# A four-layer mixer on one core: the linear-attention half's second feature block, LN1 turn, state copy and running sum move to other steps

## What is computed

```python
x = x + linear_attention(layernorm(x))   # 16 heads; q, k through softplus + 1e-6; causal running sums
x = x + ffn(layernorm(x))                # a recurrence over batches: c = f * c + i * g, then tanh(x Wo + c Uo)
x = x + softmax_attention(layernorm(x))  # causal, ALiBi
x = x + ffn(layernorm(x))
```

## Time and profile before

| what | before |
|---|---|
| median of 3 runs | 2518.53 us (2517.84 to 2527.41) |
| the profiled execution, its own time | 2519.05 us |
| its span, first to last instruction | 2517.2 us |
| PE busy | 2119.3 us (84%) |
| DVE busy | 1696.5 us (67%) |
| ACT busy | 1264.0 us (50%) |
| POOL busy | 773.3 us (31%) |
| mean granted TensorE clock | 0.938 |

### The profile page before, as it was taken

How to read it: one execution, slowest core, us unless ns; L and a number is a source line. 1 busy time by engine, 2 the same in 40 slices (tenths; PEclk the granted TensorE clock), 3 DMA queues, 4 the chain that set the end, 5 groups by cost and what they waited for, 6 DMA issues and landing times.

```text
span 2517.2 us, 58448 instructions
## 1 busy us (share of the span) xinstructions
PE 2119.3 (84%) x24737; PEld 1214.4 (48%) x24838; DVE 1696.5 (67%) x3770; ACT 1264.0 (50%) x2040; POOL 773.3 (31%) x654
## 2 busy tenths in 40 slices
PE   4678888979798885669789999999999999998953
PEld 2556555656556553334345455444544545444432
DVE  7666565665646454447878888787887887777337
ACT  3323434242434221215666676766677666766723
POOL 1234141423332011162425254243452432412110
PEclk9879999999999997878999999999999999999987
DMA  4001010101101011143323134141331412213063
GB/s 148 18 18 58 29 51 18 52 25 45 43 10 52 2 52 55 47 136 108 93 75 114 51 79 135 42 123 58 85 119 44 120 50 77 77 36 106 31 234 134
DMA packets 131540, 179.28 MB, mean 71 GB/s; under 512 B 9120, under 2 KB 95136, under 8 KB 131280
## 3 DMA queue, kind: packets, MB, share of 16 engines
q1 hardware_dynamic: 129104, 175.02, 22.6%
q10 hardware_dynamic: 2176, 0.52, 0.1%
HBM read 97.40 MB, written 77.59 MB: 70 GB/s over the span
## 4 chain that ended last, share of the span: by engine, by line
PE 64%; DVE 23%; ACT 7%; issue 4%; POOL 2%; DMA 0%; SPq 0%; DVEq 0%; POOLq 0%; ACTq 0%
PE general L897 11%; PE general L583 10%; PE out_of_heads L771 9%; DVE maxima L1462 8%; PE scores L726 6%; PE general L569 4%; PE general L908 4%; PE general L549 3%; PE turned_scores L740 3%; PE out_of_heads L657 3%; PE out_of_heads L667 2%; PE scores L615 2%; PE general L557 2%; PE out_of_heads L791 1%; PE scores L675 1%
## 5 line engine op out<-in xcount | busy, mean ns | idle before, releaser
L1462 DVE TENSOR_REDUCE maxima<-scores 128x1 f32<-128x512 f32 (+3 forms) x1536 | 796.1, 552 | 228.5 <-PE scores L702 117.2
L1095 ACT ACTIVATE probs_turned<-turned_scores 128x512 f32<-128x512 f32 x1152 | 680.0, 601 | 353.5 <-PE turned_scores L702 180.0
L726 PE MATMUL scores<-k_stacks,q_stacks 59*128 59x512 bf16 (+3 forms) x1536 | 444.7, 335 | 59.8 <-DVE maxima L1462 54.0
L740 PE MATMUL turned_scores<-q_stacks,k_stacks 61*128 61x512 bf16 (+3 forms) x1536 | 436.5, 329 | 9.4 <-ACT probs_turned L1095 9.4
L726 PEld LDWEIGHTS scores<-k_stacks,q_stacks 59*128 59x128 bf16 x1536 | 124.0, 94 | 286.8 <-DVE maxima L1462 220.0
L1792 POOL TENSOR_TENSOR ln_low<-ln 128x512 bf16<-128x512 f32 x128 | 140.8, 1107 | 278.5 <-DVE ln L1444 278.5
L1771 POOL TENSOR_SCALAR ln<-x_for_attention,ln_mean_var,ln_rstd 128x256 f32<-128x256 f32 x104 | 129.0, 1251 | 184.7 <-DVEq L1551 96.8
L1023 ACT ACTIVATE gate_tanhs<-general,feature_vectors 128x512 f32<-128x512 f32 x96 | 66.0, 687 | 204.6 <-PE general L583 200.3
L1707 POOL TENSOR_TENSOR state_low<-state_doubled,state_high 128x2048 bf16<-128x2048 f32 x14 | 57.0, 4069 | 363.0 <-ACT state_high L1029 363.0
L1063 ACT COPY values_odd_and_heads_out<-out_of_heads 128x512 f32<-128x512 f32 x64 | 37.4, 585 | 240.2 <-PE out_of_heads L667 238.5
L771 PE MATMUL out_of_heads<-probs_turned,values 128*17 128x512 f32 (+3 forms) x1536 | 154.5, 498 | 0.0
(11 more groups left out here) (262 smaller groups left out, 5322.4 us busy)
## 6 DMA issues: line engine op xcount, KB each, us to landing
x_after_attention<-x_residual SPq DMA_DIRECT2D x16, 1024.0 KB, 5.2
x_times_wo<-x_wo_out SPq DMA_DIRECT2D x64, 256.0 KB, 2.2
q_stacks<-q_stack SPq DMA_DIRECT2D x64, 256.0 KB, 4.6
k_stacks<-k_stack SPq DMA_DIRECT2D x64, 256.0 KB, 4.8
x_for_attention<-in_x SPq DMA_DIRECT2D x8, 1024.0 KB, 5.4
x_residual<-in_x SPq DMA_DIRECT2D x8, 1024.0 KB, 5.4
x_for_attention<-x_after_attention SPq DMA_DIRECT2D x8, 1024.0 KB, 5.4
ffn_h<-x_times_wo SPq DMA_DIRECT2D x32, 256.0 KB, 5.9
```

The costliest lines, as they stand in the source:

```text
L726: mx = pe.matmul(bank_s[:, first * P:(first + tiles) * P], QS[at_s:at_s + QROWS, r, i * P:(i + 1) * P], KS[at_s:at_s + QROWS, r, k0 * P:(k ...
L740: ex = pe.matmul(bank_t[:, first * P:(first + tiles) * P], KS[at_t:at_t + KROWS, r, j * P:(j + 1) * P], QS[at_t:at_t + KROWS, r, i0 * P:(i ...
L1095: nc.scalar.activation(PR[:, s % SLOTS, :], TB[s % 2][:, :], ACT.Exp).then_inc(sem["ex_taken"], 1)
L1462: r = dve.tensor_reduce(MP[:, gg % 2, g, at:at + 1], max_bank[m][:, first * P:(first + tiles) * P], AX.X, ALU.max)
```

## The change

Four things move in phase 1, and nothing is added or taken away but one split of a copy into two.

1. The second feature block's queries and keys go from k=29..36 to k=41..48 on PE, with ACT's copies and `softplus` (k=31..40 to 43..53) and DVE's `phi` (k=37 and 42 to 49 and 56). V2 and V3 take the place before them (k=37..40 to 33..36 on PE, 39 and 41 to 35 and 37 on DVE).
2. The high part of the first layer norm is turned at the end of the stage before (PE k=141, 142, ACT 142, DVE 143), waiting for the norm alone; the low part follows at k=1, 2.
3. `state_high` goes from the end of a stage to k=19 and 21 of the next, in two halves, and `state_low` on POOL behind `split_q(nb, 0)`.
4. `sum_chunk` goes from j=5 to j=10, just before `chunk_out`, `keys_turned` from j=11 to j=10, and `sum_in` from j=8 to j=12.

```diff
-                if j == 5 and chunk_in(n) and n % NT < LAST:
+                if j == 10 and chunk_in(n) and n % NT < LAST:
                     sum_chunk(n)
                 if j == 10 and chunk_in(n):
                     chunk_out(n)
-                if j == 11 and chunk_in(n + 1) and (n + 1) % NT < LAST:
+                if j == 10 and chunk_in(n + 1) and (n + 1) % NT < LAST:
                     keys_turned(n + 1)
...
+                if batch_in(b + 2) and k in (141, 142):
+                    if k == 141:
+                        pe.wait_ge(sem[f"ln_norm{phase}"], 4 * norms_to(phase, "ln1", b + 2))
+                    n = k - 141
+                    turn_part(XN, XL, 0, n, general_for(("act", "dve")[n], ("xt_act", "xt_dve")[n]))
                 if batch_in(nb):
-                    if 1 <= k <= 4:
-                        part, n = (k - 1) // 2, (k - 1) % 2
+                    if k in (1, 2):
                         if k == 1:
                             pe.wait_ge(sem[f"ln_low{phase}"], 4 * norms_to(phase, "ln1", nb))
-                        turn_part(XN, XL, part, n, general_for(("act", "dve")[n], ("xt_act", "xt_dve")[n]))
-                    for e, k0 in ((0, 5), (1, 29)):
+                        turn_part(XN, XL, 1, k - 1, general_for(("act", "dve")[k - 1], ("xt_act", "xt_dve")[k - 1]))
+                    for e, k0 in ((0, 5), (1, 41)):
...
-                    for c0, k0 in ((0, 25), (2, 37)):
+                    for c0, k0 in ((0, 25), (2, 33)):
...
-                    for e, k0 in ((0, 7), (1, 31)):
+                    if k == 2:
+                        turned_in(XT1, 1)
+                    for e, k0 in ((0, 7), (1, 43)):
...
-                            first = (9, 18, 33, 38)[2 * e + n]
+                            first = (9, 18, 45, 51)[2 * e + n]
...
-                    if k == BATCH - 1 and b < B:
-                        state_high()
+                if batch_in(b + 2) and k == 142:
+                    turned_in(XT1, 0)
+                if batch_in(pb - 1) and k in (19, 21):
+                    half = (k - 19) // 2
+                    if half == 0:
+                        act.wait_ge(sem["gate_used"], w.next("gate_used"))
+                    i = nc.scalar.copy(CP[0][:, half, :], CS[:, half, :])
+                    if half:
+                        i.then_inc(sem["state_high"], 1)
...
+                if batch_in(fb) and k == 143:
+                    turned_in(XT1, 0)
                 if batch_in(nb):
-                    if k in (3, 5):
-                        turned_in(XT1, (k - 3) // 2)
-                    places = (27, 29, 39, 41) if nb else (14, 16, 39, 41)
+                    if k == 3:
+                        turned_in(XT1, 1)
+                    places = (27, 29, 35, 37) if nb else (14, 16, 35, 37)
                     if k in places:
                         plain_values_in(nb, places.index(k))
-                    if k in (13, 22, 37, 42):
-                        phi(nb, (13, 22, 37, 42).index(k))
+                    if k in (13, 22, 49, 56):
+                        phi(nb, (13, 22, 49, 56).index(k))
...
-                if j == 8 and chunk_in(n) and n % NT < LAST:
+                if j == 12 and chunk_in(n) and n % NT < LAST:
                     sum_in(n)
...
+                if batch_in(pb - 1):
+                    state_low(1, pb - 1)
                 if batch_in(pb):
                     layer_norm(1, 2, XR, pb)
...
-                if batch_in(pb) and pb < B - 1:
-                    state_low(1, pb)
```

More of the change, by code:

```diff
@@ L1176, in fill @@
                         act.preload_act_table_set("natural_log_exp_and_others")
-                    if k in (2, 4):
-                        turned_in(XT1, k // 2 - 1)
-                    for e, k0 in ((0, 7), (1, 31)):
+                    if k == 2:
+                        turned_in(XT1, 1)
+                    for e, k0 in ((0, 7), (1, 43)):
                         if k in range(k0, k0 + 8, 2):
```

## The result

The changed kernel takes 2555.93 us (median of 4 runs, 2550.89 to 2560.71) against 2522.69 us of the kernel before in the same runs: ratio 1.0132, 95% interval 1.0097 to 1.0167. It is 33 us slower; the forecast was 2529 and the range ended at 2541. The profiled execution has a span of 2549.1 us, 31.9 more than before.

What follows compares the result with a forecast made beforehand. PE's waits, largest 56.1 us for `own_mask`, were taken as the bound. Stages 1 to 6 +19.4, filling +4 and emptying -13 gave +10.4 on 2519.05: 2529 us, range 2498 to 2541.

Steps and rivals of the forecast that it cites:

- the gain at the stage's start: First query product starts 4.6 us after `own_scores`, not 6.8: 1.55 us saved in stages 2 to 6, plus 0.6 for clock.
- the price of the sum's move: `sum_chunk` falls behind V2 of its chunk instead of into a wait: 0.45 us; 0.46 more counted at the stage's start.
- the clock in chunk 3: After PE idles some 4.4 of 4.9 us before `own_scores` of chunk 3, a lower clock adds 0.5 us.
- +3.8: Stages 2 to 6, before V0: second instruction of `phi` r=1 waits out POOL's `state_low`, 3.8 us each; bounds 0 and 4.8.
- -4.4 + 1.75 = -2.65: V0 to `chunk_out` 2: two `phi` and their wait leave, 4.4 us saved; low clock after PE's idling costs 1.75.
- +2.5: `chunk_out` 2 to `own_scores` 3: ACT's copy and logarithm, `phi` r=2 and normalising take 9.0 us instead of 6.50.
- The filling with stage 0: Stage -1: `keys_turned` comes near 69 us, 8 later; stage 0 gives back about 4; net +4 us.
- the emptying: Stages 7 and 8: `chunks_low` goes first, so PE's waits for it shrink: 13 us back, bounds 9 and 15.
- the third rival: Clock stays low longer after the new wait before chunk 3: 2.1 us more in six stages, 2542 us; chance 0.13.
- POOL did not wait for DVE: Rival: `state_low` starts behind `phi`, so five stages keep 3.8 + 1.75 us: 2501 us, faster; chance 0.20.
- the clock did not stay up: Rival: no clock losses before V0 and before chunk 3: 2517 us; chance 0.12.
- The lock for a whole instruction: Rival: first instruction of `phi` r=3 waits out POOL's `split_q`, 1 to 3 us in six stages: about 2541 us; chance 0.05.

Runs made afterwards that it cites:

- the wait for `phi`: Changed kernel plus a POOL wait that holds `state_low` until `phi` r=1 is done: 2539.57 us, ratio 1.0059 to the kernel before.
- part 2 alone: Kernel before with only the turning of LN1's high part moved to the end of the stage before: 2504.58 us, ratio 0.9937.
- The wait for the gates: Changed kernel plus a POOL wait that holds `chunks_low` until the previous stage's last state update: 2536.62 us, ratio 1.0050 to the kernel before.
- Part 1 alone: Kernel before with only the second block's queries and keys moved later and V2 and V3 earlier: 2524.16 us against 2521.73, ratio 1.0012.
- two waits on POOL, with parts 1 and 4 left out: Kernel before with LN1's and the state's moves, `chunks_low` waiting for the gates and `state_low` for `phi` r=1: 2493.38 us against 2524.69, ratio 0.9875.

## Why the prediction was wrong

Right in direction, wrong in size. Three terms of the sum were mis-sized: the gain at the stage's start, which a collision took away that the prediction did not see; the price of the sum's move; and the clock in chunk 3. By places of stage 3, the forecast's terms and what came:

| from, to | forecast | measured |
|---|---|---|
| `own_scores` 0, `chunk_turned` 0 | -1.55 - 0.6 = -2.15 | +0.33 |
| `chunk_turned` 0, V0 | +3.8 | +3.73 |
| V0, `chunk_out` 2 | -4.4 + 1.75 = -2.65 | -3.39 |
| `chunk_out` 2, `own_scores` 3 | +2.5 | +1.67 |
| `own_scores` 3, `own_scores` 4 | +1.8 + 0.45 + 0.5 = +2.75 | +4.74 |
| rest of the stage | 0 | +0.13 |
| sum | +4.25 | +7.21 |

The 0.45 is the sum's move; the prediction does not say in which chunk it falls, and it is put with chunk 3 here. Stages 1 to 6 together were to lose 19.4 us and lost 36.2.

**What held.** `phi` r=1 beside `state_low` took 4.96 us (forecast near 5), V0 waited 4.96, and the wait for `phi` brought both to 1.22. A low clock followed V0's wait (0.92 in that stretch against 0.97). The masks' 5.79 us wait shrank to 0.61, and 2.38 us came before chunk 3's `own_scores`. `chunks_low` is waited for 3.4 us. `keys_turned` of stage 0 came at 69.81. The filling with stage 0 cost 2.7 (forecast 4), and from stage 7's first `own_scores` to the end of phase 1 9.5 us came back (forecast 13, bounds 9 and 15).

**The start of the stage failed:** "I count 1.55 us for each of stages 2 to 6", and 0.6 for the clock. Laying out DVE's list I let the gates take their old time. I moved `chunks_low` forward in POOL's list for the emptying, and did not ask what it would then run beside in the full stages. The gain was there, and larger (3.1 us with part 2 alone, at full clock); the collision with the gates' second instruction, 0.68 to 2.38 us, and the low clock behind it took all of it. The wait for the gates gave it back. The rest of the layout held: the first query product, forecast 4.6 us after `own_scores`, came 6.12 after it in the changed kernel and 4.43 with that wait.

**The sum's move failed:** "`sum_chunk` falls behind V2 of its chunk instead of into a wait: 0.45". The sentence names the cover and prices it at 0.45 once per stage; another 0.46 stands in the 1.55 of the start. That is 0.9 us a stage, some 5 us in all. In stage 3 leaving the waits cost 2.0 us, in chunks 0, 1 and 3; stages 2 to 6 lost 2.1 to 4.5 each, the clock included. Alone the part measured 18, and 14 of them go with the place on PE.

**Chunk 3's clock was undersized.** "For the clock after that I add 0.5". Part 1 alone makes chunk 3 4.3 us longer at 0.82, where the forecast had 1.8 + 0.5 for it. That is the third rival, the clock staying low longer, at about its price of 2.1 us a stage. Its gains in chunks 1 and 2 were undersized by as much, so that part 1 as a whole came out near the forecast (about +4; measured +2.4) was luck.

By parts the forecast was about +4, -14, +15 and +5, with the sum's 0.46 at the start counted to part 4; alone they measured +2, -17, +26 and +18. The other rivals fell. POOL did not wait for DVE, and the clock did not stay up. The lock for a whole instruction, for which the Trainium skill, page "SBUF — State Buffer", section "Who interferes with whom", was named, did not show: the first instruction of `phi` r=3 took 0.68 us beside `split_q` in stage 3, and at most 1.42 in any run, where one POOL instruction takes 2.84 or more. Of the longer span 2.5 us lie behind phase 1, where nothing was changed; they stay unassigned.

Two readings in the prediction were off. PE's largest waits in the kernel before also include 41.1 us for POOL's `ln_low` and 20.3 us before `own_scores`, which bears on no term; and its first query product starts 7.0 us after `own_scores`, not 6.8, which is worth 0.2 us a stage.

## What to carry to other kernels

When an instruction moves out of a list, ask of everything behind it what it was held back by and what it will now run beside: here POOL's next subtraction came 8 us earlier in the stage and met the gates. A short product that stands in a wait is free only there; count the waits that it fills in every chunk before moving it. A change in several parts should be timed part by part: two waits on POOL, with parts 1 and 4 left out, turned a loss of 33 us into a gain of 31.

## What the runs showed of the hardware

A DVE instruction with two inputs in SBUF that starts after POOL's subtraction does nearly all its work behind it. The gates' instruction ended 0.55 us after `chunks_low` (408.70 and 408.15), `phi`'s 1.08 after `state_low` (435.71 and 434.63), while alone they take 0.69 and 1.22. POOL pays little: 2.27 us for 1.89, and 4.47 for 4.08. The Trainium skill, page "SBUF — State Buffer", section "Who interferes with whom", says that such a VectorE instruction contends with a GpSimd one that reads SBUF; these rows agree. Beside POOL's `split_q`, which reads SBUF too, the same `phi` instruction took 1.23 us in stage 3, and POOL's two instructions 6.32 us for 5.67: there POOL paid. With the wait for `phi` r=1, where it started 0.6 us into the second of POOL's two instructions (at 459.63), it took 2.02:

```profile
460.24 2.02 DVE L1446 TENSOR_TENSOR q_stacks<-qk_block,ffn_h 128x1024 f32<-128x1024 f32 x1
```

```profile
456.81 6.09 POOL L1755 TENSOR_SCALAR probs_turned<-qk_block,mask_even_odd 128x1024 f32<-128x1024 f32 x2
```

So which POOL instruction it is matters, and when the two meet, and the runs do not say why.
